# Spline attention as one program over all head pairs, with the turned probabilities as stationary operand and division and projection inside the pipeline

## The reference

```
q, k, v = proj(Wq), proj(Wk), proj(Wv)
sim  = einsum('bhnd,bhdm->bhnm', q, k) / sqrt(32)
xs   = clip(sim, -6, 6)
kan  = base_w * silu(xs) + einsum('...k,k->...', b_splines(xs), coef)
attn = softmax(kan, axis=-1)
out  = einsum('bhnm,bhmd->bhnd', attn, v)
return einsum('bihw,ci->bchw', out, Wo)
```

## Time and profile before

| | |
|---|---|
| median of 3 runs | 8172.36 us (8170.03 to 8176.77) |
| the profiled execution, its own time | 8168.91 us |
| its span, first to last instruction | 8166.7 us |
| mean granted clock of TensorE | 0.944 of 2.4 GHz |
| busy share of PE, PEld, DVE, ACT, POOL | 79%, 48%, 78%, 69%, 66% |

### The profile page before, as it was taken

How to read it: one execution, slowest core, us unless ns; L and a number is a source line. 1 busy time by engine, 2 the same in 40 slices (tenths; PEclk the granted TensorE clock), 3 DMA queues, 4 the chain that set the end, 5 groups by cost and what they waited for, 6 DMA issues and landing times. The chain is left out here.

```text
span 8166.7 us, 163535 instructions
## 1 busy us (share of the span) xinstructions
PE 6481.2 (79%) x52568; PEld 3958.8 (48%) x52568; DVE 6371.5 (78%) x9272; ACT 5610.8 (69%) x8624; POOL 5404.1 (66%) x3590
## 2 busy tenths in 40 slices
PE   5676778989858888886888888688888867888886
PEld 3444536767634444443444444344444434444444
DVE  3324294444459999996999999499999969999997
ACT  4425002222249999995999999389999958999996
POOL 3305000000049999995999999399999959999995
PEclk7778789999979999997999999899999989999998
DMA  1001000000020000001000000200000010000001
GB/s 65 20 6 34 0 0 0 0 0 0 0 56 0 0 0 0 0 0 33 0 0 0 0 0 0 64 1 0 0 0 0 0 32 1 0 0 0 0 0 40
DMA packets 44711, 72.23 MB, mean 9 GB/s; under 512 B 8928, under 2 KB 40448, under 8 KB 42016
## 3 DMA queue, kind: packets, MB, share of 16 engines
q1 hardware_dynamic: 41296, 70.25, 3.2%
q10 hardware_dynamic: 3288, 0.33, 0.0%
HBM read 50.69 MB, written 19.73 MB: 9 GB/s over the span
## 5 line engine op out<-in xcount | busy, mean ns | idle before, releaser
L1396 POOL TENSOR_TENSOR a_s<-a_s,a_v 128x784 f32<-128x784 f32 x1568 | 2910.1, 1856 | 349.8 <-ACT a_s L1580 349.8
L1433 PE MATMUL a_right_sides<-a_s,diag_d 128*128 128x392 f32 x6272 | 2306.1, 511 | 9.2 <-POOL a_s L1396 5.1
L1433 PEld LDWEIGHTS a_right_sides<-a_s,diag_d 128*128 128x128 f32 x6272 | 1140.7, 192 | 1166.8 <-issue 297.2
L1512 DVE SCALAR_TENSOR_TENSOR a_kan<-a_s,spline_c,a_kan 128x784 f32<-128x784 f32 x1568 | 1620.1, 1033 | 82.7
L1389 POOL TENSOR_TENSOR a_inner<-a_inner,a_x 128x784 f32<-128x784 f32 x784 | 1458.5, 1860 | 0.0
L1571 ACT ACTIVATE a_v<-a_a 128x784 f32<-128x784 f32 x1568 | 1331.5, 851 | 1.0
L1580 ACT ACTIVATE a_s<-a_v 128x784 f32<-128x784 f32 x1568 | 1330.4, 851 | 0.0
L1445 PE MATMUL a_turned<-ident,a_prob 128*112 128x128 f32 x5488 | 884.6, 284 | 536.3 <-ACT a_probT L1587 529.8
L1422 PE MATMUL a_scores<-a_K,a_q 32*64 32x392 f32 x6272 | 711.9, 523 | 521.0 <-DVE a_kan L1494 391.5
L1555 ACT ACTIVATE a_scores<-a_x 128x784 f32<-128x784 f32 x784 | 649.5, 828 | 533.6 <-DVE a_x L1485 531.8
L1485 DVE TENSOR_SCALAR a_x<-a_scores 128x392 f32<-128x392 f32 x1568 | 872.1, 557 | 131.4 <-PE a_scores L1422 131.4
(11 more groups left out here) (180 smaller groups left out, 6596.5 us busy)
## 6 DMA issues: line engine op xcount, KB each, us to landing
rows<-bias_rows_dram SPq DMA_DIRECT2D x112, 91.0 KB
X<-in_x_dram SPq DMA_DIRECT2D x4, 1568.0 KB, 16.5
v_dram<-V SPq DMA_DIRECT2D x14, 448.0 KB, 3.1
a_K<-k_dram SPq DMA_DIRECT2D x8, 784.0 KB, 9.5
QO<-q_dram SPq DMA_DIRECT2D x8, 784.0 KB, 12.7
a_V<-v_dram SPq DMA_DIRECT2D x4, 1568.0 KB, 22.3
f_R<-rinv_dram SPq DMA_DIRECT2D x8, 784.0 KB, 7.7
out_dram<-X SPq DMA_DIRECT2D x4, 1568.0 KB, 10.2
```

Source lines behind the costliest of these rows:

```text
L1396: eng.tensor_tensor(s, s, v, ALU.mult).then_inc(cubed, 1)
L1433: mm = eng.matmul(up[:, j, 0:SUB], steps[i][:, :], cubes[g][:, SUB * j:SUB * (j + 1)], start=(i == 0), stop=(i == 1))
L1512: eng.scalar_tensor_tensor(F, banked((s1, s2)[j][g][:, :]), c[:, 3 + j:4 + j], F, ALU.mult, ALU.add).then_inc(left_added, 1)
```

## The change

`attention3` now projects both images first and then runs one `kan_attention3` over all four pairs of heads, 196 blocks, with `pipeline_pairs` in place of `pipeline`: the lags run out only once, after the last block. `finish_pair3` is gone.

- SP loads q of each block straight into the buffer that PE reads, two blocks ahead at most; K and V have two buffers each, and those of the next pair are loaded at the seventh block of a pair. V now has 65 columns for two heads, the last of them ones.
- `weigh` has the turned probabilities of both heads as stationary operand (112 keys x 128 queries) and moves V (65 columns): 4 products where there were 8. The result lies by query, with the sum in its last column.
- `invert` on DVE inverts that column (128x1). `place` on ACT scales each head's 64x32 part into `by_query` (128x64, zero elsewhere). `fold_heads` on PE multiplies it by a fixed matrix, which turns it to 64 channels by 64 queries. `keep_o` on ACT copies this out. `project_out` on PE multiplies with Wo (2 products of 64 columns), and `add_output` on DVE adds 2x64 columns to X.
- X is stored in pieces from inside the program.

```
-            for pair in range(2):
-                with ExitStack() as st:
-                    buf = lambda name, shape: st.enter_context(nc.sbuf_tensor(f"{name}_{b}{pair}", shape, F32))
-                    QO = buf("QO3", [P, L])
-                    kan_attention3(nc, m, b, pair, k, QO)
-                    finish_pair3(nc, m, b, pair, k, QO)
+        kan_attention3(nc, m, k, out)
...
+                    if T >= 2:
+                        sp.wait_ge(s_made, 4 * (T - 2) + 12)
+                    for j in range(2):
+                        sp.dma_start(q[T % 2][VW * j:VW * (j + 1), :], k3.q_dram[bb][VW * pair:VW * (pair + 1), QT3 * t:QT3 * (t + 1)]).then_inc(q_ready, 16)
...
-                            for h in range(2):
-                                mm = eng.matmul(op[VW * h:VW * (h + 1), 0:QT3], V[:, k, h, :], probT[(r + ch) % 2][:, j, QT3 * h:QT3 * (h + 1)],
-                                                start=(k == 0), stop=(k == TILES - 1))
+                            mm = eng.matmul(op[:, :], probT[(r + ch) % 2][:, j, :], V[p % 2][:, k, :], start=(k == 0), stop=(k == TILES - 1))
...
+                def project_out(eng, t, r, p):
+                    eng.wait_ge(o_ready, t + 4)
+                    eng.wait_ge(x_added, t + 4)
+                    eng.wait_ge(right_gated, 4 * t + 16 if not isinstance(t, int) else min(4 * t + 16, 4 * BLOCKS3 + 1))
+                    rows = slice(VW * (p % 2), VW * (p % 2 + 1))
+                    for f in range(HALVES):
+                        mm = eng.matmul(yp[:, f, :], m.WT[rows, W_O3 + f, :], o[rows, :], start=True, stop=True)
+                    mm.then_inc(y_made, 1)
...
+                def add_output(eng, t, r, p):
+                    eng.wait_ge(y_made, t + 2)
+                    X = m.X[:, HALVES * (p // 2):HALVES * (p // 2 + 1), bass.ds(QT3 * (t - TILES3 * p), QT3)]
+                    eng.tensor_tensor(X, X, yp, ALU.add).then_inc(x_added, 1)
+
+                def invert(eng, t, r, p):
+                    eng.wait_ge(weighed, 7 * t + 9)
+                    eng.reciprocal(rinv[:, :], op[:, VW:V1]).then_inc(inverted, 1)
...
+                def place(eng, t, r, p):
+                    eng.wait_ge(inverted, t + 1)
+                    eng.wait_ge(heads_folded, t + 1)
+                    for h in range(2):
+                        rows, cols = slice(QT3 * h, QT3 * (h + 1)), slice(HD3 * h, HD3 * (h + 1))
+                        eng.activation(by_query[rows, cols], op[rows, cols], ACT.Copy, scale=rinv[rows, :]).then_inc(placed, 1)
```

More of the change, by code:

```diff
@@ L173, in conv_preact_kernel @@
         group_norm_stats(nc, m, "3")
[L174 to L182, removed]
+        attention3(nc, m, out)
 def load_and_turn(nc, m, a):
@@ L1181, with pipeline_pairs, edge, attention3 @@
 VW = 2 * HD3
-def attention3(nc, m):
+V1 = VW + 1
+PAIRS3 = 2 * B
+BLOCKS3 = PAIRS3 * TILES3
+def pipeline_pairs(eng, stages):
+    lags = max(lag for _, lag in stages)
+    def edge(k):
+        for fn, lag in stages:
+            if 0 <= k - lag < BLOCKS3:
+                fn(eng, k - lag, (k - lag) % 2, (k - lag) // TILES3)
+    head = lags + lags % 2
+    turns = (TILES3 - head) // 2
+    for p in range(PAIRS3):
+        first = TILES3 * p
+        for k in range(first, first + head):
+            edge(k)
+        with eng.Fori(0, turns) as i:
+            for k in (first + head, first + head + 1):
+                for fn, lag in stages:
+                    fn(eng, 2 * i + (k - lag), (k - lag) % 2, p)
+        for k in range(first + head + 2 * turns, first + TILES3):
+            edge(k)
+    for k in range(BLOCKS3, BLOCKS3 + lags):
+        edge(k)
+def attention3(nc, m, out):
     with ExitStack() as outer:
@@ L1193, in attention3 @@
         k.steps = [keep(f"diag_d{j + 1}", [P, P]) for j in range(2)]
[L1194 to L1197, removed]
+        k.fold = keep("fold_heads", [P, QT3])
+        k.q_dram = [dram(f"q3_dram{b}", (P, L)) for b in range(B)]
+        k.k_dram = [dram(f"k3_dram{b}", (P, L)) for b in range(B)]
+        k.v_dram = [dram(f"v3_dram{b}", (TILE, TILES, 2 * V1)) for b in range(B)]
         spline_constants3(nc, m, k)
@@ L1362, in _ @@
             def _(sp):
-                pair_rows = slice(VW * pair, VW * (pair + 1))
-                for half in range(2):
-                    sp.dma_start(K[VW * half:VW * (half + 1), :], k3.k_dram[pair_rows, :]).then_inc(loaded, 16)
-                    sp.dma_start(QO[VW * half:VW * (half + 1), :], k3.q_dram[pair_rows, :]).then_inc(loaded, 16)
-                sp.dma_start(V[:, :, :, :].rearrange("p j h c -> p j (h c)"), k3.v_dram[:, :, 2 * VW * pair:2 * VW * (pair + 1)]).then_inc(loaded, 16)
@@ L1540, in _ @@
                     (g2, l2), (g3, l3) = (((g - back) % 4, int(g < back)) for back in (2, 3))
-                    order += [(add_tanh(g3), l3), (times_x(g3), l3), (left(g3, 0), l3), (clip(g, 0), 0), (left(g3, 1), l3),
+                    order += [(add_tanh(g3), l3)] + [(invert, 3)] * (g == 1) + [(times_x(g3), l3), (left(g3, 0), l3), (clip(g, 0), 0), (left(g3, 1), l3),
                               (clip(g, 1), 0), (add_right(g3), l3), (gate(g2), l2)]
+                    if g == 1:
+                        order.append((add_output, 4))
                     if g == 2:
                         order.append((row_max, 1))
-                pipeline(dve, TILES3, order)
+                pipeline_pairs(dve, order)
             @block.scalar
@@ L1606, in _ @@
                                           (2, (copies(3), 2), (exponent(3), 2), (copies(4), 2)), (3, (copies(5), 2), (exponent(0), 1), (copies(6), 2))):
[L1607 removed]
+                    order += [(tanh((g - 2) % 4), int(g < 2))] + [(keep_o, 3)] * (g == 2) + [(magnitude(g), 0), early, (beyond(g, 0), 0), e, (beyond(g, 1), 0),
                               (squared(g, 0), 0), late, (squared(g, 1), 0)]
[L1609 removed]
```

237 lines of the change are left out of this document (114 added, 123 removed).

## The result

The changed kernel takes 7903.45 us (median of 4 runs, 7900.45 to 7905.85); the kernel before took 8171.19 on the same chip. The ratio is 0.9671 (95% interval 0.9654 to 0.9688), 268 us less. The profiled execution has a span of 7898.5 us at a mean granted clock of 0.960.

The account below looks back on a forecast made before the run. DVE was taken to set the pace: 8168.9 us less 318.7 of fixed terms plus 59 for 196 blocks longer by 0.30 gives 7909.2, as a median 7912. Range: 7875 to 7960, or 7860 to 8060 to hold 8 in 10.

Parts of the forecast that it names:

- gaps plus fills: Between pairs: three gaps go, 169.7 us less, and three pipeline fills with their drains go, 101 us less.
- The block on DVE: Each block on DVE: `add_output` adds 0.22 us and `invert` 0.08, together 0.30, between 0.17 and 0.49.
- The block on PE: Each block on PE: `weigh` takes 0.87 us, `project_out` and `fold_heads` add 0.8; busy time grows from 23.1 to 26.2.
- The second rival: PE's `weigh`: weight load never hidden, 1.52 us each, PE needs 31.1 us a block, 8518 us in all; chance 0.06.
- The cover: PE's growth costs nothing while idle time behind it covers it; without the cover, each 0.1 us a block is 20 us.
- The first rival: PE's delay gets through in the blocks: 28.7 us a block, 8046 us in all; chance 0.2.
- ACT: Each block on ACT: `place` and `keep_o` add about 0.3 us, in 2.5 us of idle time.
- The fixed terms: Outside the block's own length: gaps between pairs, fills with drains, the end and the first load, 318.7 us less in sum.
- the first load: Start of the blocks: loading K, V and q takes 17 us where it took 25.1, 8 less.
- filling, draining and ending: Pipeline fill, drain and end of the kernel: 42.3 us together, with 11.2 from the last `place` to the span's end.
- The drain: End of the kernel: 3 us for a drain in which `weigh` is longer, part of an end of 11.2 us.

Follow-up runs that it names:

- version 8: The changed kernel with `kan_attention3` called once for each pair, so loads, fills and drains between pairs come back: 8079.5 us, ratio 0.9881.
- version 3: The changed kernel with the two halves of DVE's `row_max` moved into gaps around `times_x`, where DVE waits for its own result: 7822.6 us, ratio 0.9572.
- version 4: As version 3, with `add_output` also moved into such a gap, behind the `times_x` of the third part: 7773.4 us, ratio 0.9511.
- version 5: The changed kernel with the last of a block's seven `weigh` steps issued twice, 0.86 us more PE work a block: 8093.9 us, ratio 0.990.
- version 9: The changed kernel with the first of a block's seven `weigh` steps issued twice: 7932.8 us, ratio 0.9707.
- version 10: The changed kernel with both the first and the last of a block's `weigh` steps issued twice: 7967.4 us, ratio 0.9763.
- version 1: The changed kernel with DVE's wait for the copied folded heads moved from before `add_tanh(0)` to ahead of `row_max`: 7881.8 us, ratio 0.9643.
- version 2: The changed kernel with DVE's addition of the projected block to X left out, its semaphore still raised: 7885.1 us, ratio 0.9656.

## Why the prediction was right

**Between blocks and between pairs.** Right. 191 blocks at 27.98 us across all boundaries have no step over 28.23, and version 8 prices the three boundaries at 176 us. The forecast had 270.7 (gaps plus fills) for them against the kernel before, where `finish_pair3` stood in them too; the two numbers are for different things and do not contradict each other.

**The block on DVE.** Forecast +0.30, measured 27.98 - 27.69 = +0.29. The sum was right, its parts less so: `add_output` 0.20 (forecast 0.22), `invert` 0.01 (0.08), and 0.09 for a wait that I had not counted, since it is always met. Errors of 0.09 each way cancelled, which was luck. The Trainium skill's rule (VectorE: DVE Perf Modes, The DRAIN you can't avoid) would have made 0.28 and 0.16 of the first two by their durations; the starts disagree with it, 0.20 and 0.01. The same section adds that an operation that is not held starts earlier, and the prediction left that out; these starts fit it. Versions 3 and 4 show that small instructions around `times_x` can be nearly free, so the prediction's sentence that a block can only get shorter by work taken from DVE is wrong: nothing was taken from it, and the block fell to 27.31.

**The block on PE.** `weigh` 0.865 (0.87), `fold_heads` 0.26 and `project_out` 0.59, together 0.85 (0.8). The busy time is 25.3 a block, forecast 26.2. By the starts in the same stretches, seven `weigh` took 4.4 us before, 0.62 each and not the 0.54 of rows 12, and take 6.4 now: +2.1, not +2.3; `turn` and `right_side` together take 0.7 less than before. The second rival, the weight load never hidden, is out: a load of `weigh` has a mean of 193 ns and yet an instruction takes 108. Whether loads are hidden altogether is another question. `right_side` takes 2.74 us from start to start for 8 instructions of 392 columns (3039.56 to 3042.30), so by its rate 128 columns take 0.112 (an estimate), which leaves nothing of the 0.109 of rows 11 for a load of 112 columns: there it is hidden. The Trainium skill's rule (TensorE: Matmul & The Clock Gate, Part 3, What overlaps and what doesn't), by which loads overlap only between different row groups, does not hold for rows 11. For `weigh` the 65 columns would take 0.057 by the same rate. The other 0.05 may be a load that shows in part; no run tells.

**The cover.** "PE's growth costs nothing as long as this idle time covers it" held for the change: `copies(0)` was 0.49 late, and nothing behind it was. The first rival came closer than its reason suggested. I had asked only whether PE's work fits in the block and whether ACT has room. Versions 5, 9 and 10 show another edge: 0.86 us more in one place costs 190 us, in the other 29, and most of it because the clock is down during a long `right_side`. The prediction has no term for this and took the granted clock of 1.00 as given. In the change it held: PE waits 0.93 us or more 183 times between 2500 and 7700, and no fall comes before the drain. Versions 1, 2 and 3, which give PE no more work, have four falls each there. Why the change has none is not shown, and luck may be in it.

**ACT.** `place` takes 0.60 and not some 0.2: its two activations on 64 partitions take 0.28 each, where one copy on 128 took 0.20; ACT's growth is 0.7 and not 0.3. It was hidden all the same: ACT's wait for the clip fell from 2.5 to 1.6 a block.

**The fixed terms.** The forecast was 7909 for the profiled execution, which took 7900.45: 9 less. Against the forecast, the first load takes 11.8 and not 17 (V lands in 9.3 us with 796 KB); the projections ahead of it are 8.4 us shorter than the sum of their parts from before; the earlier layers are 3.4 us earlier, which is no part of the change; and filling, draining and ending take 51.4 us and not 42.3 (33.7 less the 2.6 from the last `place` to the first DMA of `finish_pair3`, plus the 11.2). The drain is the term that was sized too small, with 3 us for its longer `weigh`: by the row above PE gets a clock of 0.52 there, and in the timeline one `weigh` takes 1.60 and one `turn` 0.85. In version 1, whose drain ran at 1.00, one `weigh` takes 0.93. The slower drain and the terms that came out shorter offset each other; the sum was close by some luck. The shorter projections are a side effect; 5.5 of the 8.4 us come from the scalings, 6.50 in each projection before and 3.73 now. The timeline of DVE shows the second one, against the earlier trace rows:

```profile
2307.00 3.73 DVE L1287 TENSOR_SCALAR xn<-X,rstd,nbias 128x3136 f32<-128x3136 f32 x2 [3.34 <-PEq L124]
```

## What to carry to other kernels

If a hand-ordered pipeline is cut at a boundary, price the cut as fill plus drain plus load: here 59 us each, 176 in all. On the engine that sets the pace read the distance of starts, and put small instructions where it waits for its own result: this was worth 130 us here. Before adding work to an engine with idle time, look at which wait it lengthens: 0.86 us before one wait cost 190 us, in another place 29. Then look at the granted clock, for a fall of it can cost more than the work that was added.

## What the runs showed of the hardware

- The granted clock of TensorE falls from 2.4 to 1.2 GHz also where PE is busy for some 90% of its time (518.3 of 560 us in version 5, 523.8 in version 9): for about 3.5 us in version 5 (0.64 over 4.8 us) and about 7 in version 9 (0.71 and 0.61 over 5 us each). Before the falls that I read PE had waited 0.94 us (version 9), 1.05 (version 2), 1.68 (version 5). Such a wait is not sufficient: version 5 has a wait of over 1.5 us in nearly every block and a fall in every second, the change has 183 waits of 0.93 us or more and no fall. Nor is a long one needed: version 10 has falls with no wait over 0.9. What decides stays open.
- Two 128x3136 scalings on DVE took 3.73 us together, in each of the two projections, where they were 6.50. Before, one of the two took 4.7 us and the other 1.9, and a memset of 3.08 us on POOL ran beside them; now both take 1.9, and the memset 0.20. That POOL is the cause was not tried by itself.
- A semaphore wait that was met long ago cost 0.09 us a block between short instructions on DVE, and nothing in another place (version 1).
